# Edge-attention kernel on one core: the first edge pass with 26 columns added by one-hot products and sixteen landed by GpSimd, and relation rows of two columns added by one block-diagonal product

## What is computed

```
scores = sum(q[dst] * (k[src] + relation[edge_type]), per head) / SCALE     # 8 heads of 16
w      = exp(scores - segment_max(scores, dst))
out    = segment_sum(w * v[src], dst) / segment_sum(w, dst)
out    = out @ Wo + bo
```

## Time and profile before

| what | value |
|---|---|
| median of 3 runs | 8024.5 us (8020.83 to 8024.66) |
| profiled execution, its own time | 8015.14 us |
| its span, first to last instruction | 8013.4 us |
| mean granted TensorE clock | 0.691 of full |
| busy share of the span: PE, PEld, DVE, ACT, POOL | 36%, 30%, 58%, 18%, 46% |
| first edge pass | about 1185 to 2850 us |
| overflow turns in it | 41 |

### The profile page before, as it was taken

How to read it: one execution, slowest core, us unless ns; L and a number is a source line. 1 busy time by engine, 2 the same in 40 slices (tenths; PEclk the granted TensorE clock), 3 DMA queues, 4 the chain that set the end, 5 groups by cost and what they waited for, 6 DMA issues and landing times. The chain is left out here.

```text
span 8013.4 us, 112882 instructions
## 1 busy us (share of the span) xinstructions
PE 2909.3 (36%) x28649; PEld 2368.4 (30%) x28650; DVE 4677.0 (58%) x10839; ACT 1435.1 (18%) x3773; POOL 3668.7 (46%) x4402
## 2 busy tenths in 40 slices
PE   4189633455555523344223432345200000001344
PEld 3168512344444422243223431334200000000122
DVE  9677345566666646687567764677544444444333
ACT  0123100111111112222112221344311111110000
POOL 0155224443333324565445544544466666563655
PEclk9999986676777766677566765666655555555677
DMA  0034223344434423345334443334332231222334
GB/s 21 10 92 108 58 75 96 96 105 101 101 88 96 92 59 70 80 83 77 67 75 83 84 69 64 77 74 73 53 51 51 52 52 51 49 51 55 77 83 80
DMA packets 293996, 576.70 MB, mean 72 GB/s; under 512 B 137262, under 2 KB 182043, under 8 KB 273827
## 3 DMA queue, kind: packets, MB, share of 16 engines
q0 software_dynamic: 113232, 255.82, 21.2%
q1 hardware_dynamic: 142642, 278.18, 11.3%
q10 hardware_dynamic: 38049, 41.86, 1.7%
HBM read 479.10 MB, written 29.32 MB: 63 GB/s over the span
## 5 line engine op out<-in xcount | busy, mean ns | idle before, releaser
L2992 PE MATMUL bank<-tab,oh 128*128 128x136 bf16 x11700 | 906.9, 251 | 704.3 <-PEq L2984 383.6
L2992 PEld LDWEIGHTS bank<-tab,oh 128*128 128x128 bf16 x11700 | 876.7, 113 | 765.2 <-issue 765.2
L1422 PE MATMUL bank<-ident,hid 128*128 128x128 f32 x125 | 55.8, 446 | 2622.7 <-PEq L1421 1482.1
L1422 PEld LDWEIGHTS bank<-ident,hid 128*128 128x128 f32 x125 | 22.7, 181 | 2669.4 <-issue 2669.4
L2735 POOL DMA_INDIRECT land_a<-table,idx_a x624 | 653.5, 1047 | 228.4 <-issue 166.4
L2754 POOL DMA_INDIRECT land_r<-table,idx_r x492 | 507.5, 1031 | 215.5 <-issue 148.4
L2915 ACT ACTIVATE rows<-bank 128x408 f32<-128x408 f32 x936 | 398.0, 514 | 848.6 <-ACTq L2914 640.2
L2841 DVE TENSOR_TENSOR prod<-prod 128x128 f32<-128x128 f32 (+4 forms) x621 | 536.5, 864 | 14.6
L2571 PE MATMUL bank<-tab_l,oh_l 128*128 128x128 bf16 x3846 | 407.5, 241 | 222.1 <-PEq L2534 102.0
L2827 DVE TENSOR_TENSOR prod<-rows,bank 128x5376 f32<-128x5376 f32 x75 | 431.6, 5755 | 61.1 <-DVEq L2826 30.5
L3218 PE MATMUL bank<-tab_l,oh_l 128*128 128x384 bf16 x1250 | 263.8, 381 | 454.9 <-PEq L3212 333.3
(11 more groups left out here) (515 smaller groups left out, 8530.2 us busy)
## 6 DMA issues: line engine op xcount, KB each, us to landing
loc<-el_loc SPq DMA_DIRECT2D x78, 1088.0 KB
loc_l<-el_loc SPq DMA_DIRECT2D x52, 1088.0 KB
typ_l<-el_typ SPq DMA_DIRECT2D x52, 672.0 KB
rows_r<-land_r SPq DMA_DIRECT2D x123, 272.0 KB
landings_l<-landings_l SPq DMA_DIRECT2D x41, 784.0 KB
attr<-in_edge_attr ACTq DMA_DIRECT2D x75, 343.8 KB
land_a<-table,idx_a POOLq DMA_INDIRECT x936
land_r<-table,idx_r POOLq DMA_INDIRECT x492
```

Of the source, the lines that this page charges most:

```text
L2992: last = pe.matmul(got[g % full][:, (c - of[0]) * W1:(c - of[0] + 1) * W1], oh[:, o], tab[:, t, x], start=n == 0, stop=n == len(parts) - 1 ...
```

## The change

It changes what is fetched how. In the first edge pass only the 26 narrow columns are still fetched by one-hot products. The eight wide columns are fetched by GpSimd as the eight first overflow columns are, so that sixteen columns are landed (`LAND` = 16). The relation rows of two neighbouring columns are added by one product: the even column's type one-hot lies in partitions 0 to 63, the odd one's in 64 to 127 (`TH` = 21 pairs), and `rel3` is block-diagonal, 256 columns wide, in three bf16 parts. The key groups are four landed and two narrow ones of 4 as early keys, and three of 4 and three of 2 after; the value groups are twelve of 2 or 3 columns. The list-building stage stores the wide columns' indices ahead of the overflow list, and the types in pair order.

```diff
-        el_ovf = dram("el_ovf", [RMAX + 1, P, 2 * LISTW], I32)
+        el_ovf = dram("el_ovf", [RMAX + 1, P, NW + 2 * LISTW], I32)
...
+                        dve.tensor_tensor(two_rows, in_pairs[0], in_pairs[1], ALU.add).then_inc(ch.semaphore, ch.one())
...
+            TH = MC // 2
+            FC = NB + 1
+            LAND = MC - FC
...
-            oh, oht = bb("oh", [P, OHC, P], BF16), bb("oht", [P, MC, P], BF16)
-            rel3 = bb("rel3", [P, 2, D], BF16)
+            oh, oht = bb("oh", [P, FC, P], BF16), bb("oht", [P, TH, P], BF16)
+            rel3 = bb("rel3", [P, 3, 2, D], BF16)
...
-            wide = [range(c, min(c + 4, PC)) for c in range(NB + 1, PC, 4)]
-            narrow = [range(c, c + 4) for c in range(NB - 7, NB + 1, 4)] + [range(c, c + 3) for c in range(0, NB - 7, 3)]
-            landed_groups = [range(PC + c, PC + c + HALF) for c in range(0, FIRST, HALF)]
-            key_groups = landed_groups + wide + narrow
-            value_groups = [range(max(c - BANKC, 0), c) for c in range(PC, 0, -BANKC)]
+            narrow = [range(c, c + 4) for c in range(FC - 8, FC, 4)] + [range(c, c + 4) for c in range(6, FC - 8, 4)] + [range(c, c + 2) for c in range(0, 6, 2)]
+            landed_groups = [range(c, c + HALF) for c in range(FC, MC, HALF)]
+            key_groups = landed_groups + narrow
+            VG = 2 * len(banks)
+            value_groups = [range(FC * (n - 1) // VG, FC * n // VG) for n in range(VG, 0, -1)]
...
                         for k in range(2):
                             sp.dma_start(typ[k * TYPES:(k + 1) * TYPES],
-                                         el_typ[bass.ds(r, 1), 0:MC].rearrange("r j p -> (r j p)").partition_broadcast(TYPES)).then_inc(s("typ_in"), 16)
+                                         el_typ[bass.ds(r, 1), k * TH:(k + 1) * TH].rearrange("r j p -> (r j p)").partition_broadcast(TYPES)).then_inc(s("typ_in"), 16)
...
-                        for c in range(FIRST):
+                        for c in range(LAND):
                             pool.indirect_dma_start(land_a[:, c, :], None, source,
...
-                        for k in range(1, WIDE):
-                            dve.tensor_scalar(oh[:, PC + (k - 1) * NW:PC + k * NW].rearrange("p c n -> p (c n)"), loc[:, (NB + 1) * P:],
-                                              iota_k[:, k:k + 1], None, ALU.is_equal).then_inc(ch.semaphore, ch.one())
...
-                    def type_rows(c, to, first, last):
-                        for x in range(2):
-                            done = pe.matmul(to, oht[:, c], rel3[:, x], start=first and x == 0, stop=last and x == 1, skip_group_check=True)
+                    def type_rows(n, of):
+                        for c in range(of[0], of[0] + len(of), 2):
+                            for x in range(3):
+                                pe.matmul(keys_of(n)[:, c - of[0]:c - of[0] + 2], oht[:, c // 2], rel3[:, x], start=c == of[0] and x == 0, stop=False, skip_group_check=True)
```

More of the change, by code:

```diff
@@ L1091, in _ @@
                     dve.memset(loc_f[:], 0.0).then_inc(ch.semaphore, ch.one())
+                    dve.memset(type_p[:], float(TYPES)).then_inc(ch.semaphore, ch.one())
                     dve.memset(base[:], 0.0).then_inc(ch.semaphore, ch.one())
@@ L2100, in l0_pass @@
             tiles = [min(BANKC, NB - g) for g in range(0, NB, BANKC)]
-            wide = [range(c, min(c + 4, PC)) for c in range(NB + 1, PC, 4)]
-            narrow = [range(c, c + 4) for c in range(NB - 7, NB + 1, 4)] + [range(c, c + 3) for c in range(0, NB - 7, 3)]
-            landed_groups = [range(PC + c, PC + c + HALF) for c in range(0, FIRST, HALF)]
-            key_groups = landed_groups + wide + narrow
-            value_groups = [range(max(c - BANKC, 0), c) for c in range(PC, 0, -BANKC)]
+            narrow = [range(c, c + 4) for c in range(FC - 8, FC, 4)] + [range(c, c + 4) for c in range(6, FC - 8, 4)] + [range(c, c + 2) for c in range(0, 6, 2)]
[3 more added lines that the diff above has]
+            value_groups = [range(FC * (n - 1) // VG, FC * n // VG) for n in range(VG, 0, -1)]
             AHEAD = len(banks)
-            assert len(key_groups) % len(banks) == 0 and len(value_groups) % len(banks) == 0
-            assert sorted(c for of in key_groups for c in of) == list(range(MC))
-            assert sorted(c for of in value_groups for c in of) == list(range(PC))
+            assert all(of[0] % 2 == 0 and len(of) % 2 == 0 for of in key_groups)
             def keys_of(n):
@@ L2209, in gathers @@
                                 pool.sem_inc(s("land_r_free"), -1)
-                                pool.tensor_copy(idx_r[:], run_now[:].rearrange("p (k s) -> p k s", k=2)[:, :, bass.ds(i * MORE + FIRST, MORE)]).then_inc(ch.semaphore, ch.one())
+                                pool.tensor_copy(idx_r[:], run_now[:, NW:].rearrange("p (k s) -> p k s", k=2)[:, :, bass.ds(i * MORE + FIRST, MORE)]).then_inc(ch.semaphore, ch.one())
                                 copied()
@@ L2250, in onehots @@
                         dve.sem_inc(s("loc_in"), -16)
[L2251 to L2254 removed]
+                        dve.tensor_scalar(oh[:].rearrange("p c n -> p (c n)"), loc[:], iota_p[:], None, ALU.is_equal).then_inc(ch.semaphore, ch.one())
                         dve.wait_ge(ch.semaphore, ch.count)
@@ L2350, in main_chunk @@
                         onehots()
-                        dve.tensor_tensor(by_head(kp[:, PC:]), by_head(va[:]), wt[:, PC:MC].unsqueeze(3).broadcast_to([P, FIRST, HEADS, V]), ALU.mult).then_inc(ch.semaphore, ch.one())
+                        dve.tensor_tensor(by_head(kp[:, FC:]), by_head(va[:]), wt[:, FC:MC].unsqueeze(3).broadcast_to([P, LAND, HEADS, V]), ALU.mult).then_inc(ch.semaphore, ch.one())
                         dve.wait_ge(ch.semaphore, ch.count)
@@ L2549, in keys @@
                             bank_for(n)
[L2550 to L2552 removed]
+                            type_rows(n, of)
+                            if of[0] >= FC:
                                 if n == 0:
@@ L2562, in keys @@
                                     pe.sem_inc(s("land_a_free"), 1)
-                                    pe.sem_inc(s("bank_full1"), 1)
+                                    pe.sem_inc(s(f"bank_full{n}"), 1)
                                 else:
-                                    done.then_inc(s("bank_full0"), 1)
+                                    done.then_inc(s(f"bank_full{n}"), 1)
                                 continue
                             for c in of:
-                                for m, (o, t) in enumerate(pieces(c)):
+                                parts = [(o, t, x) for o, t in pieces(c) for x in range(3)]
+                                for m, (o, t, x) in enumerate(parts):
                                     tile_ready(ready, t)
-                                    for x in range(3):
-                                        pe.matmul(keys_of(n)[:, c - of[0]], oh[:, o], tab[:, t, x, 0:D], start=m == 0 and x == 0, stop=False, skip_group_check=True)
-                                done = type_rows(c, keys_of(n)[:, c - of[0]], False, True)
+                                    done = pe.matmul(keys_of(n)[:, c - of[0]], oh[:, o], tab[:, t, x, 0:D], start=False, stop=m == len(parts) - 1, skip_group_check=True)
                             done.then_inc(s(f"bank_full{n % len(banks)}"), 1)
```

56 lines of the change are left out of this document (29 added, 27 removed).

## The result

The changed kernel takes 8197.6 us (8167.7 to 8206.1) against 8022.7 us: ratio 1.0218, 95% interval 1.0196 to 1.0241, some 175 us slower. The forecast was slower by 75 us; the measured time lies inside its range (7970 to 8250), in the upper part. The profiled execution has a span of 8204.4 us.

The account below looks back on a forecast made before the run. No engine is full; a chain through GpSimd's gathers, whose landing slows TensorE, bounds the kernel. One-turn runs +27, runs with more turns +42 and list building +6 sum to +75 us, giving 8100 us, range 7970 to 8250.

Parts of the forecast that it names:

- Gathers: Runs with one turn: eight more first gathers on GpSimd lengthen the chain by 10.5 us per run.
- landed groups: Runs with one turn: TensorE's four landed groups instead of two, ahead of the gathers, add 4.0 us (bounds +1.0 to +7.1).
- TensorE after the release: Runs with one turn: once gathers have landed, TensorE has less left to do, -9.4 us per run (-7.9 and -13).
- price of 3.5 instructions per us: Assumed TensorE rate while gathers land: 84 instructions done in 24 us, leaving 45 products, 3.6 us, for afterwards.
- first rival: TensorE does nothing in the added slow time, so -9.4 becomes +1.3 per one-turn run; 8320 us in all, chance 0.12.
- It is neither the bandwidth nor the issuing, it is the landing of gathers: Claim that landing of GpSimd's gathers slows TensorE, about tenfold at worst, since it did 76 products in 4 us during issuing.
- VectorE in the chain: Runs with one turn: shorter type one-hots, values and one-hots on VectorE save 3.3 us per run.
- Runs with more turns: Ten runs with two or more turns: terms sum to +4.2 us each, +42 us together (bounds +10 to +90).
- term of -4.4 for the values: Runs with more turns: values fall from 9.7 to 5.3 us, mostly done before the second turn's gathers (bounds 0 and -5.4).
- lower bound of +10 us for these runs: Low end of the forecast for the ten runs with more turns together, whose central value was +42 us.
- List building: One more VectorE operation of 0.25 us in each of 25 runs while building the lists: +6 us.
- The hold doesn't grow with the gathers: Faster rival: eight more gathers don't lengthen TensorE's slowing, so only savings remain; -76 us, 7950 us, chance 0.22.

## Why the prediction came out too low

The direction and the chain were right, the sum was not. Means over runs 11 to 24 of the traces, from one-hots to one-hots, before to after (in brackets the kernel with eight of the sixteen gathers); each part runs from the start or end of a row of one line to that of the next:

```
run with one turn                 before  [minus 8]  after   measured  forecast
landed products, index copy         7.2     9.3       9.8      +2.6      +4.0
first gathers                      11.8    11.3      21.3      +9.5     +10.5
turn's gathers                      9.7     9.7       9.7       0         0
last gather to first value product 14.2     7.4       8.7      -5.5      -9.4
first value product to one-hots    15.4    13.5      13.6      -1.8      -3.3
sum                                58.3    51.3      63.1      +4.8      +1.8
```

- *Gathers* and *landed groups*: right in kind, +12.1 where +14.5 was forecast.
- *TensorE after the release*, -9.4: **this step failed**. The sum put 1.6 + 3.6 = 5.2 us from the last gather to the first value product; it is 8.7. The release was left at 1.6 us after the last gather, and TensorE's products follow one another again only 4.4 us after it (mean of runs 11 to 24): 2.8 of the 3.9 us that are missing. The products left then take 4.3 us and not 3.6, and the stretch before was 14.2 and not 14.6.
- The price of 3.5 instructions per us was wrong too, though 37 of the 81 products are left and its own working gives 39 (it says 45, but 162 - 84 = 78 instructions are 39 products). That is luck. In the trace the node update is done 10.3 us after the first gather, 37 key products follow one behind the other, and then 18.2 us of hold let 7 through. With eight gathers fewer it is 41, then 7 in 7.0 us, and 34 left: 11 us more of hold let nothing more through. So the gain of -6.8 comes from TensorE's shorter program, which puts the node update and half of the later keys ahead of the hold, and the eight more gathers take 1.3 back. The mechanism of the first rival, nothing is done in the added slow time, is what these two kernels show; its 8,320 was too high because it let the gain of the shorter program fall with it.
- *"It is neither the bandwidth nor the issuing, it is the landing of gathers"*: the part on the issuing is refuted. Gathers with a gap land just the same and hold nothing. The 76 products in 4 us stood at the start of a train of gathers (first at 2364.30), where TensorE isn't slowed yet; its first idle time without a wait in that train reads

```profile
2370.09 0.28 PE L2571 MATMUL bank<-tab_l,oh_l 128*128 128x128 bf16 x2 [0.47 <-issue]
```

- *VectorE in the chain*, -3.3: measured -1.8. The types' 0.7 and the one-hots' 1.1 are there; the values' 1.3 isn't: on fewer columns they still take 5.2 to 6.0 us, since they now wait for TensorE.
- *Runs with more turns*, +4.2: measured +9.7 us per run in runs 0 to 9. By parts, means of runs 1 to 9: first gathers +10.1; last gather to first value product +1.2 (forecast -0.6), since the release comes 3.2 us after the last gather's issue where it came 2.0; values to one-hots -3.1 (forecast -6.4); one-hots to the first gather +2.1 (forecast +1.2). **The term of -4.4 for the values is the second that failed.** Its 9.7 us was read from one of the three slowest runs, the mean of runs 0 to 9 is 8.7, and they now take 7.3 and not 5.3: a saving of 1.3. The lower bound of +10 us for these runs doesn't follow from the terms either: 10 - 0.6 - 0.8 - 5.4 is +3.2 per run, +32.
- *List building*, +6: not seen, the pass begins 4 us earlier.
- Together: 97 us in runs 0 to 9 where 42 were forecast, 74 in runs 10 to 23 where 1.8 each gave 25.
- *The hold doesn't grow with the gathers* (7,950) is refuted; the hold does depend on something that rival left open, the distance between gathers. The Trainium skill, SBUF — State Buffer, section "SBUF: two separate sides", was weighed against the trace in the forecast. The traces now agree with it as far as data goes: copies and plain DMAs that move twice the bytes hold nothing. What holds are indirect DMAs without a gap, whatever they carry.

What stays open is through what a train of gathers holds other engines. The Trainium skill, DMA: Bandwidth & Descriptors, section "SWDGE vs HWDGE vs iDMA", says that GpSimd writes the descriptors of its DMAs into rings in SBUF; it counts plain and indirect ones alike. Since 28 plain ones in 16 us held nothing (262 products, 16.4 per us), the writing of descriptors as such doesn't explain the hold, and no run here shows what does.

## What to carry to other kernels

Find what an engine waits for before pricing its work: TensorE was slowed by another engine's instruction train, and one tiny memset with its wait, 0.6 us behind each gather, gave the kernel before 2.7%. A stretch that is to clear a suspect must lie well inside its work and not at the start: in the first 4 us of a train of gathers nothing is held. Work laid into a stretch in which an engine is slowed counts as not done until a row shows it finished and seen. Take a term from the mean of all runs of its kind; and once a hold is taken away, look at who is the chain then: the changed kernel only exchanged TensorE's hold for GpSimd's own time.

## What the hardware showed unexpectedly

- Gathers 1.26 us apart let some 60 to 90 products of TensorE through at full rate and in the end about one in 2 us, whatever the products' width, the loop's length, the rows' width or their number (128 or 64). At 1.87 us apart, with a memset and its wait between, there is no loss at all.
- VectorE is held too: small memsets at under 3 per us in place of 21; ScalarE less, 4.8 activations per us in place of 6.0.
- Plain DMAs started by GpSimd 0.53 us apart, and SyncE's copies at 200 GB/s, hold nothing.
- After 48 gathers without a gap TensorE is free only 7.8 us after the last issue, after 24 it is 4.2 us.
